# A two-layer gated transformer block on one core: order of the first maximum rows, a value bias folded into the projection, and one batch split in three pieces

## The reference, cut to what matters

```
x = x + tanh(g_xattn[0]) * xattn0(layernorm(x), ctx)
x = x + tanh(g_ffn[0])   * moe0(layernorm(x))
x = x + tanh(g_xattn[1]) * xattn1(layernorm(x), ctx, ctx)
x = x + tanh(g_ffn[1])   * moe1(layernorm(x))

# xattn0, 16 heads of 8 columns
q, k, v = heads(x @ Wq + bq), heads(x @ Wk + bk), heads(x @ Wv + bv)
y  = softmax(causal(q k^T / sqrt(8))) v
qc, kc, vc = heads(x @ Wcq + bcq), heads(ctx @ Wck + bck), heads(ctx @ Wcv + bcv)
y += softmax(qc kc^T / sqrt(8)) vc
return y @ Wp + bp
```

## Time and profile before

| | |
|---|---|
| median of three runs | 379.35 us (378.6, 379.35, 382.72) |
| the profiled execution, its own time | 382.61 us |
| its span in the profile | 380.8 us |
| PE busy | 334.8 us (88%) |
| DVE busy | 233.1 us (61%) |
| ACT busy | 190.3 us (50%) |
| POOL busy | 109.7 us (29%) |
| share of PE in the chain that ended last | 72% |
| share of DVE, ACT, DMA in it | 10%, 6%, 5% |

### The profile page before, as it was taken

How to read it: one execution, slowest core, us unless ns; L and a number is a source line. 1 busy time by engine, 2 the same in 40 slices (tenths; PEclk the granted TensorE clock), 3 DMA queues, 4 the chain that set the end, 5 groups by cost and what they waited for, 6 DMA issues and landing times.

```text
span 380.8 us, 6988 instructions
## 1 busy us (share of the span) xinstructions
PE 334.8 (88%) x2646; PEld 194.7 (51%) x2646; DVE 233.1 (61%) x538; ACT 190.3 (50%) x387; POOL 109.7 (29%) x201
## 2 busy tenths in 40 slices
PE   4779849999999999788889799999986698899994
PEld 2446514434334343344366576777765366565663
DVE  5797858888888888456442143322204579538765
ACT  3366238897888978557358322222347132314220
POOL 5527003144442433223585004433360101100000
PEclk9899958999999999899989899999998699969999
DMA  7779993030305005130161560000004000000000
GB/s 171 181 191 211 211 217 84 24 143 2 114 20 152 4 2 170 48 123 2 26 210 33 139 165 18 18 19 17 8 22 113 0 2 1 2 0 0 29 1 28
DMA packets 35635, 27.80 MB, mean 73 GB/s; under 512 B 5436, under 2 KB 32880, under 8 KB 35602
## 3 DMA queue, kind: packets, MB, share of 16 engines
q1 hardware_dynamic: 33718, 25.34, 26.5%
q0 software_dynamic: 1280, 1.88, 1.5%
q10 hardware_dynamic: 604, 0.14, 0.2%
HBM read 11.89 MB, written 5.26 MB: 45 GB/s over the span
## 4 chain that ended last, share of the span: by engine, by line
PE 72%; DVE 10%; ACT 6%; DMA 5%; issue 4%; POOL 2%; ACTq 1%; SPq 0%; POOLq 0%; DVEq 0%
PE psum L1451 13%; PE psum L1650 11%; PE psum L1681 7%; PE psum L1634 6%; PE psum L1669 4%; PE psum L1417 4%; PE psum L1393 4%; PE psum L1385 3%; PE psum L1469 3%; ACT ot_sb L805 2%; DVE nmax L1026 2%; PE psum L1395 1%; DMA qcat<-nmax_t 1%; PE psum L1743 1%; PE psum L1420 1%
## 5 line engine op out<-in xcount | busy, mean ns | idle before, releaser
L1026 DVE TENSOR_REDUCE nmax<-psum 128x2 f32<-128x1024 f32 (+2 forms) x88 | 103.8, 1217 | 20.1 <-PE psum L1393 11.9
L830 ACT ACTIVATE parts<-psum 128x512 f32<-128x512 f32 (+1 forms) x88 | 44.7, 569 | 9.2 <-PE psum L1417 8.5
L1169 DVE TENSOR_TENSOR qcat<-psum,qk_r 128x320 f32<-128x320 f32 x32 | 15.7, 491 | 44.7 <-ACT qk_r L871 44.6
L1650 PE MATMUL psum<-p_more,kcat 128*128 128x320 f32 x128 | 41.8, 468 | 0.7 <-DVE p_more L1160 0.7
L727 POOL DMA_INDIRECT rows_back<-qcat,back_at x24 | 22.9, 954 | 54.6 <-ACT qcat L862 49.8
L871 ACT ACTIVATE qk_r<-psum 128x320 f32<-128x320 f32 x32 | 14.0, 438 | 47.8 <-PE psum L1650 47.8
L1681 PE MATMUL psum<-h_t,kcat 128*128 128x512 f32 x64 | 31.9, 626 | 0.7 <-ACT h_t L841 0.7
L1393 PE MATMUL psum<-kcat,qcat 64*128 64x512 bf16 x128 | 25.4, 394 | 5.8 <-DVE nmax L1026 5.2
L1650 PEld LDWEIGHTS psum<-p_more,kcat 128*128 128x128 f32 x128 | 22.9, 197 | 13.9 <-issue 5.2
L1417 PE MATMUL psum<-qcat,kcat 64*128 64x256 bf16 x256 | 25.7, 280 | 3.3 <-ACT p_more L830 1.2
L1451 PE MATMUL psum<-parts,v_aug 128*9 128x256 f32 (+1 forms) x352 | 28.2, 366 | 0.0
(11 more groups left out here) (220 smaller groups left out, 607.5 us busy)
## 6 DMA issues: line engine op xcount, KB each, us to landing
kcat<-parts SPq DMA_DIRECT2D x18, 192.0 KB, 5.8
qcat<-parts SPq DMA_DIRECT2D x24, 128.0 KB, 5.1
kcat<-ones_b SPq DMA_DIRECT2D x8, 192.0 KB, 5.1
kcat<-in_L_ffn_wi_gate_dram SPq DMA_DIRECT2D x6, 256.0 KB, 3.3
kcat<-in_L_ffn_wi_up_dram SPq DMA_DIRECT2D x6, 256.0 KB, 3.8
kcat<-in_L_ffn_wo_dram SPq DMA_DIRECT2D x6, 256.0 KB, 4.6
parts<-in_L_ffn_w_dram SPq DMA_DIRECT2D x3, 512.0 KB, 5.4
rows_in<-zeros SPq DMA_DIRECT2D x1, 1290.0 KB, 5.7
```

The costliest lines, as they stand in the source:

```text
L830: act.activation(p_slots[u % NPT][:, 0:w], s2_bank(s2_place[u])[:, 0:w], ACT.Exp, scale=SCALE).then_inc(p_in, 1)
L1026: dve.tensor_reduce(dst[:, :, n * g:n * (g + 1)], src.rearrange("p (r q k) -> p r q k", r=PAR, q=n), AX.X, ALU.max, negate=True).then_inc( ...
L1169: dve.tensor_tensor(hh[:, e % 2, f, 0:SLOTS], bank(3 + 2 * (i % 2))[:, 0:SLOTS], sg[:, i % 2, 0:SLOTS], ALU.mult).then_inc(hh_in[0], 1)
L1650: ins = pe.matmul(bank(2 + 2 * (i % 2) + m)[:, 0:SLOTS], w_t[e][:, m, f * P:(f + 1) * P], xs_t[:, e % 2, :], start=True, stop=True)
```

## The change: what it does

Four edits. SP's order becomes: pad 0, layouts of batch 0, layouts of batch 1, pad 1, pad 2, row 0, layouts of batch 2, row 1, late loads, pad 3, layouts of batch 3, row 2. The product that adds the value bias in each `v` job is taken out; in its place ACT spreads bv over 128 columns, one product with `w_p` (a new last job, `bv`) makes bv @ Wp in all rows, ACT copies it out, and POOL adds it to `b_p`. `w_p` is loaded by ACT among the early loads instead of by SP among the late ones. DVE splits batch 1 in three pieces, each as soon as its projection is taken.

```diff
-            load_late: load(w_p[:, :], a["L0_xattn_Wp"])
...
+            lay_out_batch(1)
             pad(1)
-            lay_out_batch(1)
             pad(2)
-            pad(3)
-            lay_out_batch(2)
             zero_rows = [(rows_in, ZW), (rows_back, 4 * D)]
             for n in range(NPART):
...
                 if n == 0:
-                    lay_out_batch(3)
+                    lay_out_batch(2)
                 if n == 1:
                     load_late()
+                    pad(3)
+                    lay_out_batch(3)
...
@@ POOL, add_bias
+                link(pool.tensor_tensor(b_p[:, :], b_p[:, :], bp_v[:, :], ALU.add))
                 link(pool.tensor_scalar(bp_g[:, :], b_p[:, :], tanh_g[:, 0:1], None, ALU.mult))
...
@@ ACT, loads behind job k 0, and the jobs
                     load(w_v[:, :], a["L0_xattn_Wv"])
-                    load(b_v[DC:DC + 1, :], a["L0_xattn_bv"].unsqueeze(0))
+                    load(bv_col[:, :], a["L0_xattn_bv"].unsqueeze(1))
                     load(w_cv[0:DC, :], a["L0_xattn_Wcv"])
                     load(w_cv[DC:DC + 1, :], a["L0_xattn_bcv"].unsqueeze(0))
+                    load(w_p[:, :], a["L0_xattn_Wp"])
...
+                if (kind, i) == ("v", 2):
+                    act.wait_ge(in_w, 16 * N_IN_W)
+                    act.wait_ge(zero_in, 2)
+                    act.activation(bv_wide[:, :], zeros[:, 0:D], ACT.Identity, bias=bv_col[:, :]).then_inc(wide_in, 1)
...
+                elif kind == "bv":
+                    act.activation(bp_v[:, :], src[:, 0:D], ACT.Copy).then_inc(job_act, 1)
...
@@ DVE
             for b in range(1, SPLIT_DVE):
-                dve.wait_ge(job_act, taken_count(job_at("ck", b)))
-                split(b, 0, XW, True)
+                for job, first, end in (("q", 0, QW), ("k", QW, QW + S), ("ck", QW + S, XW)):
+                    dve.wait_ge(job_act, taken_count(job_at(job, b)))
+                    split(b, first, end, job == "ck")
...
@@ PE, project
-                        pe.matmul(dst[:, t * P:(t + 1) * P], h_t[:, tok:tok + P], w_v[:, :],
-                                  start=True, stop=False)
-                        ins = pe.matmul(dst[:, t * P:(t + 1) * P], c_t[DC:DC + 1, 0:P], b_v[DC:DC + 1, :],
-                                        start=False, stop=True)
+                        ins = pe.matmul(dst[:, t * P:(t + 1) * P], h_t[:, tok:tok + P], w_v[:, :],
+                                        start=True, stop=True)
+                elif kind == "bv":
+                    pe.wait_ge(wide_in, 1)
+                    ins = pe.matmul(dst[:, 0:D], bv_wide[:, :], w_p[:, :], start=True, stop=True)
```

More of the change, by code:

```diff
@@ L83, in flamingo_gated_kernel @@
         b1_col = sb("b1_col", [P, 1])
-        b_v = sb("b_v", [DC + 1, D])
+        bv_col = sb("bv_col", [P, 1])
+        bv_wide = sb("bv_wide", [P, D])
+        bp_v = sb("bp_v", [P, D])
         b_p = sb("b_p", [P, D])
@@ L226, in flamingo_gated_kernel @@
         in_w = sem("in_w")
+        wide_in = sem("wide_in")
         in_late = sem("in_late")
@@ L326, in flamingo_gated_kernel @@
             jobs += [("v", b), ("cv", b)]
+        jobs.append(("bv", 0))
         JOB_RING = (4, 5, 6)
@@ L404, in flamingo_gated_kernel @@
         KV1_BANK = [2, 3, 4, 5] * 2
-        N_IN_LATE = 11
-        N_IN_WCK, N_IN_WQ, N_IN_W = 2, 6, 6
+        N_IN_LATE = 10
+        N_IN_WCK, N_IN_WQ, N_IN_W = 2, 6, 7
         UNITS1 = [(s, e) for s in range(NHT) for e in range(E)]
@@ L512, in load_late @@
             def load_late():
-                load(w_p[:, :], a["L0_xattn_Wp"])
                 load(b_p[:, :], a["L0_xattn_bp"].partition_broadcast(P))
```

## The result

The changed kernel ran at 375.29 us (median of four, 374.63 to 376.0), the kernel before beside it at 380.77 (four, 378.6 to 382.72): ratio 0.9892, 95% interval 0.9849 to 0.9935. The ratios leave out executions in a slower state, in which the profile shows a lower granted clock and a time some per cent longer, so a ratio need not be the quotient of two medians given beside it. The gain is about 1%, where 1.9% of the shown median was forecast. The profiled execution took 376.0 us, its span 374.2.

What follows compares the result with a forecast made beforehand. PE, 72% of the chain, idled 4.53 us for row 0's late DMA, then ran at half clock. Gains of 7.2 us at step 0 and 8.4 at step 6 left 7.2 at step 24: 372.2 us from 379.35, range 370.3 to 376.4.

Steps and rivals of the forecast that it cites:

- The row: Row 0: issued at 42.6 into an empty queue, lands at 45.1; step 0 at 45.4 instead of 52.61, 7.2 us.
- Rival (d): Row 0 still meets a backlog: 6.3 us to land, step 0 at 49.0, gain 3.6, 376 us; chance 0.10.
- The pieces: DVE's split of batch 1: 6.22 us against 4.74 in one, ending 24.60 against 24.47; gains nothing by itself.
- The loads: ACT's early loads: w_p moves the eviction at 14.50 and PE's next projections by 0.4 us (0.3 to 0.6).
- The clock: Second pass, first six steps: full rate, step 6 at 52.3, 8.4 us gained (7.2 to 8.6).
- Rival (c): Clock falls all the same, PE sparsely busy from 42 to 45 us; row 2 not waiting; 372.2 to 373.4 us; chance 0.08.
- Row 2: Reached 16.3 us after row 1, 0.6 late; step 24 waits 1.1 (0 to 3.6), starts at 75.9; 7.2 us remain.
- The ring order: DMA queue before step 24: small row 2 stays behind large layouts, gain 7.2 us; by an unloaded transfer alone 8.4.
- The end: Everything behind step 24 is work of PE that shifts as it is.

Runs made afterwards that it cites:

- e_again: The changed kernel once more, with no edit; ratio 0.9914 (0.9876 to 0.9951) to the kernel before.
- e_order: The kernel before with SP's new order alone, value bias and split as before; ratio 0.9956 (0.9905 to 1.0008).
- e_bias: The kernel before with the value bias folded into the projection alone, w_p among ACT's early loads; ratio 1.0105 (1.0056 to 1.0155).
- e_whole: The changed kernel with batch 1 split in one go again; ratio 1.0002 (0.9958 to 1.0046) to the kernel before, median 381.05 us.
- e_loads: The changed kernel with ACT's early loads spread over the evictions; ratio 0.9923 (0.9886 to 0.9959) to the kernel before.
- e_warm: The changed kernel with two unused products behind each of units 14, 15 and 16; ratio 0.9941 (0.9903 to 0.9979) to the kernel before.
- e_pad3: The changed kernel with only pad 3 moved, behind the layouts of batch 2; ratio 0.988 (0.9812 to 0.9949) to the kernel before.

## Why the prediction was wrong

The time lay in the range and the sign was right, but the gain forecast, 7.2 us at step 24, was 3.8 (4.6 in e_again). Two terms failed: steps 0 to 6 at full clock, and SP's run from row 1 to row 2. Point by point:

- **The row.** Right. The turn's copy came at 42.56 (forecast 42.3), row 0 was issued at 42.86 into an empty queue, and step 0 started at 45.95 (45.4) with no wait. Rival (d) is excluded. e_order and e_bias show that neither the order nor the bias alone gives this. Some luck was in it. The queue was to be empty at 41, 1.5 us ahead of the row; the DMA share was 1.08 from 41 to 42, 0.58 from 42 to 43 and 0.03 only after that, so about 0.4 us were left. And the copy came nearly on time although ACT's loads had cost more than forecast; what made up for that, no run separates.
- **The pieces.** By the traces right that they gain nothing: the turn's copy does not move at all. The times of e_whole leave it open.
- **The loads.** The term was mis-sized: "One more (w_p) at the 0.4 us of its neighbours" stalled ACT 1.06 us more (3.46 against 2.40). The load of bv as a column took 0.64 where the row had taken 0.49, and its neighbours grew too: from the load of bv to the last gate load 3.49 us instead of 2.43. e_loads shows 2.3 us to hang on this run of loads, if the clock holds.
- **The clock.** Wrong, and the first step that failed: "PE no longer goes idle for 4.5 us, so I take the six steps at full rate". They took 8.59 us (7.90 in e_again), not 6.9. Rival (c), given 0.08, was the case. I read the earlier trace rows as a fall from full idleness; sparse work from 41.5 on was enough, and the trace of before had shown PE at 0.60, 0.39 and 0.31 us per us from 45 to 48 ahead of its fall. e_warm shows the cause, since unused work at that place keeps 2.4 GHz, and the price: 1.4 us at step 6 in the first profile and 0.7 in e_again, 1.6 and 1.1 us in the issue of row 1 (0.3 of either was there at row 0 already). Even at full rate the six steps took 7.17 us.
- **Row 2.** The place and the mechanism were right, but two terms of the sum were too small. Row 1 came at 57.19, not at 55.7; with the clock kept (e_warm) it came at 55.63. SP then needed 18.3 us to row 2, not 16.3: sixteen DMAs at 0.645 make 10.3, they took 12.24 (63.26 to 75.50), two of them 1.23 and 1.39 and one with a gap of 0.45 ahead of it. Together 1.5 + 2.0 = 3.5 us, which is the forecast's error at step 24 (79.34 against 75.9). The landing was as forecast there, 3.7 us from issue. In e_again the error of 2.7 us is made up otherwise: 1.0 in row 1, 0.9 in SP's run, 0.8 in the landing (4.5). In both SP came to the row late, by 2.4 and 1.5 us, where 0.6 was forecast.
- Rival (c) said "row 2 then not waiting". That was wrong: SP works from row 1 to row 2 without a pause (16.9 to 18.3 us in the six profiles with this order), so a delay of row 1 moves row 2 along and hides nothing. The clock's loss and SP's add up.
- **The ring order.** I put the wait down partly to the queue full of layouts, with the rule of the Trainium skill ("DMA: Bandwidth & Descriptors", section "Queues, rings and completion order") that a queue is served in ring order. No run contradicts the rule, but it did not decide: e_pad3 keeps twelve layouts ahead of the row and has no wait; what counted was that SP reached the row late. The queue had its part only then: the row landed 3.7 and 4.5 us after its issue, where step 0, which needs row 0, started 3.1 us after the issue of that row into an empty queue. The 2.4 us of the earlier trace rows, which I set beside a landing of 6.3, end with the last bytes moved and not with the landing.
- **The end.** From step 33 on nothing changed, as forecast. The 2.8 us that the profiled spans differ by there arise in parts that the change doesn't touch, and by the granted clock they are the clock's.

What stays open: why e_whole's times are 1% above what its trace and that of the changed kernel let expect, and so whether the pieces are worth anything; which of SP's issues take twice their time, and why, as they fall elsewhere in each run; and why PE stood idle 2.4 to 2.7 us ahead of 22 us in two of the three runs with spread loads and 1.09 in the third.

## What to carry to other kernels

When a transfer is moved ahead of others in the program of the engine that issues them, add up that engine's own time to the next transfer that somebody waits for, and compare it with the distance between the two: here 16.3 us forecast against 15.7 was a wait by design, and four DMAs moved into a gap removed it. Removing a wait of PE need not bring its clock back if what remains there is sparse work. One profile shows one case of the clock and of the issuing engine: the same kernel a second time split its error between them otherwise. A part of a change that relieves an engine in front of a fixed wait gains nothing until the wait is gone, and can cost: the bias alone, with its loads, was 1% slower.

## What the runs showed of the hardware

- The granted clock fell with PE at work 0.31 to 0.58 us of each us from 41.5 to 44.2, not only in idleness. With products filling 43 to 46 us (e_warm) it stayed, through 0.59, 0.48 and 0.48 us of work in the three us after them too. The low clock then lasted 10.2 us in the changed kernel's first profile, 6.8 in e_again and 3.4 in e_whole (row 0 copied at 42.56, 42.62 and 42.55).
- The same list of DMAs from row 1 to row 2 took SP 18.3, 17.2, 18.1, 16.9 and 17.1 us to issue (changed kernel, e_again, e_whole, e_warm, e_loads): most take 0.65 us, single ones 0.8 to 1.45.
- After a wait of about 2 us at step 24, PE having been busy before, the clock fell in e_again, e_warm and e_loads (steps 24 to 27 in 5.74, 5.74 and 5.84 us) and not in the changed kernel's first profile or in e_whole (4.39 us each). The same wait may cost 1.4 us more or not.
- The record of the clock can miss a spell: from 16 to 20 us the changed kernel's profile grants 1.00, yet the four products of 256 columns at 16.29 took 2.04 us, as at half rate, against 1.10 at 21.72.
